# Attention and feed-forward layer: the last batch's output rows and two late tiles as single fp16 passes, spread over the last two pairs of heads

## The reference, cut to what matters

```
x + Attn(layernorm(x)) + FFN(layernorm(x))          # x: 4 batches, 1024 tokens, 256 wide
q, k = rotary(xn @ Wq) * DH**-0.5, rotary(xn @ Wkv)   # 16 heads of 16; k is also v
out = softmax(q k^T) v                                # per batch and head
attention = out @ Wout + bout
FFN = (silu(xn Wg^T / 127) * (xn Wu^T / 127)) (Wd^T / 127)
```

## Time and profile before

| | us |
|---|---|
| median of 3 runs (lowest, highest) | 833.54 (833.08, 833.87) |
| the profiled execution's own time | 833.63 |
| its span, first to last instruction | 831.8 |

### The profile page before, as it was taken

One profiled execution on the slowest core, in us unless ns is written; L12 is line 12 of the kernel. 1 busy time (PEld: TensorE's weight loads), 2 busy tenths in 40 slices (PEclk: granted clock), 3 DMA queues, 4 the chain that ended last, 5 costly groups with the idle time before them and its releaser, 6 DMA issues.

```text
span 831.8 us, 19133 instructions
## 1 busy us (share of the span) xinstructions
PE 799.3 (96%) x7316; PEld 296.1 (36%) x7316; DVE 736.4 (89%) x891; ACT 691.0 (83%) x1268; POOL 267.3 (32%) x504
## 2 busy tenths in 40 slices
PE   4888999999999999999999999999999999999997
PEld 2344555445333233333333333333333333333234
DVE  6776888888899999999999999999999999999702
ACT  5565455545799999999999999999999999999982
POOL 3877678886120001101222222222222222222210
PEclk9998999999999999999999999999999999999999
DMA  9455655565111111111221122221222112221222
GB/s 311 120 129 113 140 117 112 113 119 129 42 33 35 29 37 30 31 30 45 57 58 50 49 54 58 53 51 49 55 56 58 51 49 52 58 55 50 83 72 75
DMA packets 111680, 60.55 MB, mean 73 GB/s; under 512 B 71372, under 2 KB 101900, under 8 KB 111588
## 3 DMA queue, kind: packets, MB, share of 16 engines
q1 hardware_dynamic: 111588, 59.32, 28.6%
HBM read 28.57 MB, written 16.90 MB: 55 GB/s over the span
## 4 chain that ended last, share of the span: by engine, by line
PE 90%; ACT 3%; issue 2%; DVE 2%; POOL 2%; DMA 1%; SPq 0%; DVEq 0%; ACTq 0%; POOLq 0%
PE ps L753 34%; PE ps L770 19%; PE ps L735 15%; PE ps L629 9%; PE ps L643 4%; ACT arena L1014 2%; PE ps L608 1%; PE ps L607 1%; PE ps L606 1%; DMA arena<-w_up_dram 1%; PE ps L678 1%; PE ps L781 1%; PE ps L797 1%; PE ps L783 1%; PE ps L782 1%
## 5 line engine op out<-in xcount | busy, mean ns | idle before, releaser
L1169 DVE TENSOR_REDUCE negmax<-ps 128x2 f32<-128x1024 f32 x512 | 589.0, 1216 | 9.8 <-PE ps L770 6.4
L1014 ACT ACTIVATE arena<-ps 128x512 f32<-128x512 f32 x1024 | 555.5, 595 | 32.4 <-PE ps L735 10.6
L753 PE MATMUL ps<-arena 128*32 128x256 f32 x4072 | 326.5, 392 | 2.4 <-issue 2.2
L735 PE MATMUL ps<-qs,ks 51*128 51x512 f16 x1024 | 197.9, 382 | 3.3 <-ACT arena L1014 2.1
L770 PE MATMUL ps<-ks,qs 48*128 48x512 f16 x972 | 189.4, 386 | 0.0
L753 PEld LDWEIGHTS ps<-arena 128*32 128x32 f32 x4072 | 80.4, 107 | 128.0 <-issue 126.9
L770 PEld LDWEIGHTS ps<-ks,qs 48*128 48x128 f16 x972 | 46.5, 92 | 195.1 <-DVE negmax L1169 142.3
L629 PE MATMUL ps<-arena,side 128*128 128x512 f16 x384 | 92.4, 391 | 3.8 <-DVE side L1114 3.8
L1434 POOL TENSOR_TENSOR arena<-arena,x_all 128x256 f32<-128x256 f32 x22 | 16.1, 731 | 230.3 <-ACT arena L1035 230.3
L735 PEld LDWEIGHTS ps<-qs,ks 51*128 51x128 f16 x1024 | 50.7, 93 | 77.8 <-ACT arena L1014 45.7
L1365 POOL TENSOR_TENSOR mparts<-rowmax,munit 128x16 f16<-128x16 f32 x32 | 7.1, 221 | 210.3 <-DVE rowmax L1179 210.3
(11 more groups left out here) (115 smaller groups left out, 511.6 us busy)
## 6 DMA issues: line engine op xcount, KB each, us to landing
parts_d<-arena SPq DMA_DIRECT2D x64, 128.0 KB
x_all<-x_dram SPq DMA_DIRECT2D x8, 512.0 KB, 9.1
qs<-parts_d SPq DMA_DIRECT2D x64, 64.0 KB, 1.9
ks<-parts_d SPq DMA_DIRECT2D x64, 64.0 KB, 1.9
o_d<-arena SPq DMA_DIRECT2D x124, 32.0 KB
arena<-o_d SPq DMA_DIRECT2D x24, 128.0 KB
arena<-inv_d SPq DMA_DIRECT2D x48, 64.0 KB
out_dram<-arena SPq DMA_DIRECT2D x24, 128.0 KB, 1.8
```

What stands on the lines that cost most here:

```text
L735: mm = pe.matmul(ps[:, score_bank(place(p, kt, 2 * half + a)), :], ks[ring][top:top + ROWS, kt * P:(kt + 1) * P], qs[ring][top:top + ROWS, ...
L753: mm = pe.matmul(ps[32 * j:32 * j + 32, 7, cols], vstage[pl % 2][:, j % 2, kt, :], probs[PER_STEP * (kt % PBUF) + j][:, cols], start=(kt = ...
L1014: act.activation(probs[PER_STEP * (kt % PBUF) + j], ps[:, score_bank(place(p, kt, j)), :], ACT.Exp).then_inc(exp_done, 1)
L1169: dve.tensor_reduce(negmax[pl % 2][:, h, :, kt], ps[:, bank:bank + 2, :], AX.X, ALU.max, negate=True).then_inc(max_done, 1)
```

## The change

Tiles 21 and 23 are now the late ones, tile 22 takes slot 3 of pair 31. The late tiles are split like the others and their six fp16 passes each are dealt out by a table over half steps: tile 21 in slots 11 to 13 of pair 30, tile 23 in slots 5 to 8 of pair 31. The front rows are split by POOL into fp16 halves and their 24 passes (three in place of one fp32 matmul) lie in slots 7 to 10, 14, 15 of pair 30 and 0 to 2 and 10 to 13 of pair 31. The back rows are split by DVE and take 24 passes behind the last values. Their loads are parted into one of `o_d` and one of `inv_d`, and the front's is moved from the start of pair 30 into pair 29. The last 64-row matmuls alternate between upper and lower rows, and DVE's last eight adds become four of double size. The sums of a pair get a semaphore of their own, `sums_in`, so that `invert` waits for them alone; `copy_o` waits for both. One small POOL multiply scales `wlast`.

```diff
+LATE_TILES = (PAIRS - LAG - 1, PAIRS - LAG + 1)
+LATE_BANK = 3
+LATE_AT = {(PAIRS - 2, 11): (0, range(0, 2)), (PAIRS - 2, 12): (0, range(2, 4)), (PAIRS - 2, 13): (0, range(4, 6)),
+           (PAIRS - 1, 5): (1, range(0, 2)), (PAIRS - 1, 6): (1, range(2, 3)), (PAIRS - 1, 7): (1, range(3, 5)),
+           (PAIRS - 1, 8): (1, range(5, 6))}
+FRONT_AT = {(PAIRS - 2, 7): range(0, 2), (PAIRS - 2, 8): range(2, 4), (PAIRS - 2, 9): range(4, 6),
+            (PAIRS - 2, 10): range(6, 8), (PAIRS - 2, 14): range(8, 10), (PAIRS - 2, 15): range(10, 12),
+            (PAIRS - 1, 0): range(12, 14), (PAIRS - 1, 1): range(14, 16), (PAIRS - 1, 2): range(16, 18),
+            (PAIRS - 1, 10): range(18, 20), (PAIRS - 1, 11): range(20, 21), (PAIRS - 1, 12): range(21, 23),
+            (PAIRS - 1, 13): range(23, 24)}
+LAST_ORDER = [t for n in range(CT) for t in (n, n + CT)]
+PAIR_ORDER = [0, 2, 1, 3]
...
                 sp.dma_start(sums[slot % 2], osb[slot % 2][DH:DH + 32 * (PER_STEP - 1) + 1:32, :]
-                             ).then_inc(o_stored[slot % 2], 16)
+                             ).then_inc(sums_in[slot % 2], 16)
...
+                if p == PAIRS - 3:
+                    load_last_o(0, front_in)
+                    load_last_inv(0, front_in)
...
             p = PAIRS - 2
             slot(p, p, False, True)
+            sp.wait_ge(divided, CREDIT + LOOP_TILES - 1)
+            load_tile(*tile_of(LOOP_TILES)[0:2], LOOP_TILES % 2)
             p = PAIRS - 1
-            sp.wait_ge(divided, CREDIT + p - LAG)
-            load_tile(*tile_of(p - LAG + 1)[0:2], (p - LAG + 1) % 2)
             store_o(p - 1, p - 1)
-            sp.wait_ge(divided, CREDIT + p - LAG + 1)
-            load_tile(*tile_of(p - LAG + 2)[0:2], (p - LAG + 2) % 2)
+            sp.wait_ge(divided, CREDIT + LOOP_TILES)
+            load_tile(*tile_of(LOOP_TILES + 1)[0:2], (LOOP_TILES + 1) % 2)
             store_inv(p - 1, p - 1)
-            store_res(*tile_of(p - LAG))
+            for k in range(2):
+                sp.wait_ge(o_stored[k], 16 * PER_STEP * (PAIRS // 2 - k))
+            load_last_o(1, back_in)
             for k in range(2):
                 sp.wait_ge(inv_stored[k], 16 * QH * (PAIRS // 2 - k))
-            load_last(1, back_in)
-            for n in range(LOOP_TILES, (BATCH - 1) * BT):
-                store_res(*tile_of(n))
+            load_last_inv(1, back_in)
+            store_res(*tile_of(LATE_TILES[0]))
+            store_res(*tile_of(tile_in_pair(p)))
+            store_res(*tile_of(LATE_TILES[1]))
...
+            def tile_passes(n, k, bank, passes):
+
+                if passes[0] == 0:
+                    pe.wait_ge(divided, CREDIT + n + 1)
+                    if n == LATE_TILES[1]:
+                        pe.wait_ge(late_done, 1)
...
+                for i in passes:
+                    g, half = i // 3, (atile_lo if i % 3 == 2 else atile_hi)[k]
+                    mm = pe.matmul(ps[:, bank, 0:DIM], half[:, g, :], (wo_lo if i % 3 == 1 else wo_hi)[:, g, :],
+                                   start=(i == 0), stop=(i == 3 * HG - 1))
...
+                    if (p, slot) == min(FRONT_AT):
+                        pe.wait_ge(max_done, MAXES * PAIRS)
+                        pe.wait_ge(front_split, 2 * CPB)
+                    if (p, slot) in LATE_AT:
+                        i, passes = LATE_AT[p, slot]
+                        n = LATE_TILES[i]
+                        tile_passes(n, n % 2, LATE_BANK, passes)
+                    for u in FRONT_AT.get((p, slot), ()):
+                        if u == 3 * 2 * LATE_BANK:
+                            pe.wait_ge(late_done, len(LATE_TILES))
+                        last_pass(u // 3, 0, P, u % 3)
...
+            def divide_back():
+
+                dve.wait_ge(back_in, 16 * 2 * CPB)
...
+            def add_late(n):
+
+                dve.wait_ge(wout_done, CREDIT + n + 1)
+                dve.wait_ge(res_free[n % 2], 16 * (n // 2))
...
+            add_late(LATE_TILES[0])
             invert(PAIRS - 2, RING - 2)
-            for n in range(LOOP_TILES, (BATCH - 1) * BT):
-                add_late(n)
+            add_late(LATE_TILES[1])
+            divide_back()
...
+            n = LAST - LAG
+            divide(n, n % 2)
+            divide_front()
+            add_tile(n, n % 2, n)
+            split_max(PAIRS - 1, RING - 1)
+            pool.wait_ge(pv_done, STEPS * (PAIRS - 2))
+            stage_values(PAIRS - 1, BATCH - 1, RING - 1, PPB - 1)
+            for n in range(LAST - LAG + 1, (BATCH - 1) * BT):
                 divide(n, n % 2)
+            n = tile_in_pair(PAIRS - 1)
+            add_tile(n, n % 2, n)
```

More of the change, by code:

```diff
@@ L285, in build @@
         o_stored = [sem(f"o_stored{i}") for i in range(2)]
+        sums_in = [sem(f"sums_in{i}") for i in range(2)]
         inv_done = sem("inv_done")
@@ L508, in load_last, with load_last_inv @@
                     sp.dma_start(olast[k][0:rows, g, :], o_d[BATCH - 1, g, 0:rows, tok]).then_inc(landed, 16)
+            def load_last_inv(g, landed):
+                rows = P if g == 0 else BACK_ROWS
+                for k in range(CPB):
+                    tok = slice(k * CHUNK, (k + 1) * CHUNK)
                     src = inv_groups[BATCH - 1, g, 0:rows // DH, tok]
@@ L772, in maxima @@
                 mm.then_inc(max_scores, 1)
[L774 to L788, removed]
+            def tile_passes(n, k, bank, passes):
[3 more added lines that the diff above has]
+                        pe.wait_ge(late_done, 1)
+                    if n == 0:
+                        pe.wait_ge(wo_split, 3)
+                for i in passes:
+                    g, half = i // 3, (atile_lo if i % 3 == 2 else atile_hi)[k]
+                    mm = pe.matmul(ps[:, bank, 0:DIM], half[:, g, :], (wo_lo if i % 3 == 1 else wo_hi)[:, g, :],
+                                   start=(i == 0), stop=(i == 3 * HG - 1))
+                if i == 3 * HG - 1:
+                    mm.then_inc(wout_done, 1)
@@ L790, in last_out, with last_pass @@
             def last_out(t):
                 return ps[:, t // 2, (t % 2) * DIM:(t % 2 + 1) * DIM]
[L793 to L798, removed]
+            def last_pass(t, g, rows, i):
+                tok = slice(t % CT * P, (t % CT + 1) * P)
+                pe.matmul(last_out(t), osplit[t // CT][0:rows, g, i // 2, tok], (wo_lo if i == 1 else wo_hi)[0:rows, g, :],
+                          start=(g + i + t % 2 == 0), stop=False)
@@ L800, in project_back @@
             def project_back(t):
-                pe.matmul(last_out(t), olast[t // CT][0:BACK_ROWS, 1, t % CT * P:(t % CT + 1) * P], wo[0:BACK_ROWS, 1, :],
-                          start=False, stop=False)
+                for i in range(3):
+                    last_pass(t, 1, BACK_ROWS, i)
             def step(turn, ls, last_turn=False):
@@ L881, in _ @@
                 project_back(t)
-            pe.wait_ge(wo_scaled, 2)
+            pe.wait_ge(wo_split, 4)
             pe.wait_ge(normed, 1)
-            for t in range(BT):
+            for t in LAST_ORDER:
                 rows = slice(t // CT * HEAD_ROWS, (t // CT + 1) * HEAD_ROWS)
@@ L1265, in _ @@
                 step(TURNS, ls, True)
-            def divide_last(g, landed, done):
-                rows = P if g == 0 else BACK_ROWS
-                dve.wait_ge(landed, 16 * 2 * CPB)
-                for k in range(CPB):
-                    dve.tensor_tensor(olast[k][0:rows, g, :], olast[k][0:rows, g, :], ilast[k][0:rows, g, :], ALU.mult
-                                      ).then_inc(done, 1)
-            def add_late(n):
-                dve.wait_ge(wout_done, CREDIT + n + 1)
-                dve.wait_ge(res_free[n % 2], 16 * (n // 2))
-                dve.tensor_tensor(res[n % 2], ps[:, 0, 0:DIM], x_all[:, n, :], ALU.add).then_inc(late_done, 1)
-            divide_last(0, front_in, front_divided)
+            add_late(LATE_TILES[0])
             invert(PAIRS - 2, RING - 2)
-            for n in range(LOOP_TILES, (BATCH - 1) * BT):
-                add_late(n)
-            divide_last(1, back_in, back_divided)
+            add_late(LATE_TILES[1])
+            divide_back()
             dve.wait_ge(sums_turned, 1)
@@ L1419, in divide, with divide_front @@
                 pool.tensor_tensor(atile_lo[k], atile[k], atile_hi[k], ALU.subtract).then_inc(divided, 1)
+            def divide_front():
+                pool.wait_ge(front_in, 16 * 2 * CPB)
+                for k in range(CPB):
+                    pool.tensor_tensor(olast[k][:, 0, :], olast[k][:, 0, :], ilast[k][:, 0, :], ALU.mult
+                                       ).then_inc(front_divided, 1)
+                for k in range(CPB):
+                    pool.wait_ge(front_divided, k + 1)
+                    pool.tensor_copy(osplit[k][:, 0, 0, :], olast[k][:, 0, :]).then_inc(front_split, 1)
+                for k in range(CPB):
+                    pool.wait_ge(front_split, k + 1)
```

(5 more changed lines are left out.)

83 lines of the change are left out of this document (41 added, 42 removed).

## The result

| | median us | lowest, highest | runs |
|---|---|---|---|
| before | 833.43 | 833.08, 833.87 | 4 |
| changed | 841.10 | 840.07, 842.40 | 4 |

The ratio is 1.0092, 95% interval 1.0079 to 1.0105: the changed kernel is 7.7 us slower. The forecast was slower, but by 3.6 us, and the time lies above its range. The profiled execution of the changed kernel took 840.07 us, its shortest; its span is 838.2. The four times spread over 2.3 us, those of before over 0.8.

The account below looks back on a forecast made before the run. ScalarE was taken to set the pace in the pair loop, with TensorE 96% busy; 6.14 - 3.42 + 2.1 - 1.2 = +3.6 us on the median of 833.54 gave 837.1, range 834.9 to 839.3.

Parts of the forecast that it names:

- the one on pair 30: Pair 30's passes lose nothing waiting for maxima or front rows; slot 3 of pair 31 comes 0.24 us earlier.
- Tile 23's standstill: Slot 5 of pair 31: TensorE waits 6.5 us for tile 23, loaded behind pair 30's store; slot 6 is 6.14 us late.
- The clock: Behind the standstill in pair 31 the clock is at half for 5.1 us, costing 2.1 us, bounds 1.3 and 2.9.
- fourth rival: Slower still: clock takes 7 us or more to return, loads land later, or slots 10 to 13 stall; 839 to 841; chance 0.15.
- The covered waits: Pair 31: slot 10's wait for tile 23's add (near 812) and the back rows' split are hidden behind slot 5's wait.
- the rivals: The faster one: tile 23 ready for slot 5, then slot 10's wait costs 3.5 us, about 832 to 833; chance 0.08.
- The passes: Each half step on TensorE takes 0.89 us without a pass, 1.09 with one, 1.20 with two.
- from slot 6 to slot 15: Pair 31: fp16 passes in place of fp32 matmuls take 10.37 us instead of 13.79, 3.42 less.
- The tail: Behind the last values: shorter passes, alternating matmuls and four larger adds save 1.2 us, between 0.8 and 1.6.
- The loop: The extra wait in `copy_o` and the earlier `invert` cost 0 in the pair loop; upper bound 0.6 us.

Follow-up runs that it names:

- e4: Kernel before with only the front rows' four loads moved into pair 29, ahead of the transposing transfer of pair 30's maxima; 836.14 us, ratio 1.0052.
- f1: Changed kernel with the front rows' loads issued about 9 us earlier, right after the load of pair 31's queries and keys; 837.70 us, ratio 1.0058.
- e1: Changed kernel with tile 23's load ahead of the store of pair 30's products in SP's queue; 839.53 us, ratio 1.0091.
- e3: Changed kernel with the front rows' loads issued behind the transposing transfer of pair 30's maxima; 840.61 us, ratio 1.0113.
- g2: Changed kernel run once more, unedited; 839.82 us, ratio 1.0079 to the kernel before.
- f3: Changed kernel with 62 extra matmuls in slot 5 of pair 31 ahead of the wait for tile 23; 839.63 us, ratio 1.0083.
- e2: Changed kernel with tile 23's load and tile 21's store both ahead of the store of pair 30's products; 831.17 us, ratio 0.9991.
- f2: Changed kernel with tile 23's load and tile 21's store ahead of pair 30's product store, and front loads about 9 us earlier; 828.66 us, ratio 0.9956.
- f4: Kernel before with only the sums' own semaphore and the waits that go with it; 833.24 us, ratio 1.0003.
- g1: f2 with the last 64-row matmuls and the four last adds in natural order; 829.69 us, ratio 0.9964.

## Why the forecast was right in direction and too small

**The step that failed** is the one on pair 30. It followed the front's loads only to POOL ("issued in pair 29, some 8 us before") and asked whether they arrive in time. It did not ask what they delay: the transposing transfer of pair 30's maxima, which the change puts behind them in SP's queue and beside them in the DMA engines (5.3 us to land instead of 2.2), and with it the loads of the rows. It counted 0, and set pair 30's slots to start where they had. The move alone (e4) cost 1.14 us in the profiled pair, the changed kernel 1.33 in one profile and, with the clock at half behind the wait, 3.12 in another, and f1, with the same loads 9 us earlier, 0. By the median of e4 the move costs 4.2 us, more than half of the 7.7; the part of it that its profile does not have is not located.

**Tile 23's standstill** was right in place, cause and order: e1 removes it. It was 7.44 us, not 6.5. The chain from the end of the copy to the release took 9.41 (801.75 to 811.16) and not 8.46, nearly all of it in the one long issue on SP. This issue was 1.25 to 1.64 us long in the four profiles with this queue order and no extra work (after, e3, f1, g2); in e1 and f3 the store of the products was 1.0 to 1.4 us longer instead (3.26 and 2.90 for four, against 1.86), and in before, e2, e4, f2, f4 and g1 nothing was. What makes it long is not settled. In the changed kernel a fetch of instructions lies beside it (16 KB near 804.2), but the kernel before has one between 804.0 and 804.5 and no long issue.

**The clock** was right as a mechanism (f3). The term was 2.1 us with bounds of 1.3 and 2.9; measured are 1.84 twice (after, e3) and 3.39 twice (f1, g2). Time at half behind the wait was 4.5 and 8.8 us, against the 5.1 taken from two shorter idle times. The lower one is in the profiled execution, the upper one lies beyond the bound; it is the first condition of the forecast's fourth rival, "slower still". That the clock could also fall behind a shorter wait in pair 30 was not priced, since the forecast had no wait there.

**The covered waits.** That slot 10 would bind once slot 5 did not was said; its size was forecast at 3.5 us in the rivals and, with e1, at 2, and was 5.9. The store's landing was taken for 2 us, the median before; it was 4.8. The forecast also had VectorE's add of tile 23 done near 812. That add waits for tile 23's last pass in slot 8 as well, and in the changed kernel it started at 816.89, released by that pass; slot 10's passes came at 818.79, so this cost nothing.

**The passes.** A half step with two passes takes 1.21 to 1.22, forecast 1.20, and from slot 6 to slot 15 the run without a standstill (e2) gives 3.24 us less than before, forecast 3.42. **The tail** gave 0.98, forecast 1.2. **The loop** gave nothing and cost nothing (f4).

Added up for the profiled execution: 3.6 forecast, 1.33 for the rows of pair 30, 0.95 for SP's issue, 0.2 each for pair 30's slots and the tail, 0.14 in the first part, less 0.3 for the clock: 6.1 of the 6.4 measured. The other executions were 1 to 2.3 us longer. Only one more execution of this kernel, g2's, was profiled, and there both the late rows and the clock took more.

## What to carry to other kernels

- When loads are moved earlier, price what is issued behind them and what flies beside them, not only when they arrive. Here a megabyte in a quiet place of the queue cost nothing, and 9 us later it cost 1.1 to 3.1 us in the profiled pairs and 3 to 5.6 by all executions of e4, because two small transfers of the critical chain then had to be made beside it. Putting it behind the first of the two did not help.
- Before work is pulled forward, follow its inputs back through every in-order queue to the last thing that waits there. The order in the queue was the same as before; that the tile was asked for six half steps earlier turned 0 into 7.4 us. Behind one such wait there may be a second of the same size: one reordering alone gained next to nothing, both together 9.4 us of the stretch.
- A standstill of TensorE costs more than its length. In this kernel a wait of 7 us brought 1.8 to 3.4 us on top, and waits of about 1.6 us some 1.5. Look at the granted clock behind every wait, the short ones too.

## What the runs showed of the hardware that was not expected

- After a standstill of 6.98 to 7.46 us the granted clock stayed at half for 4.5 us of resumed work in two executions (after, e3) and for 8.8 in two others (f1, g2); after 5.90 us (e1) for 4.4.
- The clock also fell behind the short waits at the head of pair 30: in three profiles with waits of 1.56, 1.62 and 1.66 us, for 3.4 us each, and not in four with waits of 1.04 to 1.25.
- With a megabyte of loads issued just ahead of it, the transposing transfer landed after 5.1 to 5.7 us (after, e1, e2, e4, f3, g2), without it after 2.2 to 2.3 (before, e3, f1, f2, f4, g1).
- A 128 KB store issued right behind four loads of 192 KB each, two of them broadcasts of the inverses, needed 4.8 us to land instead of 2.0 (e1). The median of such stores behind these loads is 4.6 us there and 4.5 in the changed kernel.
- The issue of one load took SP's queue 1.25 to 1.64 us in place of 0.42, at one place only and not in all orders of the queue; this is open.
